# Context values of a cross-attention block: one VectorE subtraction for three GpSimd ones

## The reference

```python
x = x + attention(layernorm(x), ctx, ctx)      # ctx: (8, 375, 512)
x = x + experts(layernorm(x))

def attention(x, k_cache, v_cache):
    q, k_new, v_new = x @ wq.T, x @ wk.T, x @ wv.T
    k = concat([k_cache, k_new]); v = concat([v_cache, v_new])
    attn = softmax(q @ k.T * 512**-0.5)
    return (attn @ v) @ wo.T

def experts(x):                                 # gate: softmax, top 2 of 8, renormalised
    for gu, dp, w in (gate_up_proj, down_proj, combine_w):
        gate, up = split(x @ gu.T, 2)
        acc += w * ((silu(gate) * up) @ dp.T)
```

## Time and profile before

| | us |
|---|---|
| median of 3 runs | 463.65 |
| lowest and highest run | 462.8, 464.78 |
| the profiled execution's own time | 463.22 |
| its span, from the first to the last instruction | 461.4 |

### The profile page before, as it was taken

How to read it: one execution, slowest core, us unless ns; L and a number is a source line. 1 busy time by engine, 2 the same in 40 slices (tenths; PEclk the granted TensorE clock), 3 DMA queues, 4 the chain that set the end, 5 groups by cost and what they waited for, 6 DMA issues and landing times.

```text
span 461.4 us, 7183 instructions
## 1 busy us (share of the span) xinstructions
PE 443.8 (96%) x2549; PEld 376.0 (82%) x2549; DVE 346.2 (75%) x653; ACT 251.7 (55%) x409; POOL 95.8 (21%) x122
## 2 busy tenths in 40 slices
PE   8899999999999899999999999999999999999991
PEld 6878888888888578888888888888888888888870
DVE  5856646556644577998888888888888888888850
ACT  3648434524533536656656656656656656656621
POOL 4005071552425424003003003003003003003002
PEclk9999999999999999999999999999999999999996
DMA  8975994505544464955956946856856946856203
GB/s 237 396 229 150 290 238 138 167 23 145 195 137 189 123 224 115 344 199 200 268 172 194 277 167 200 270 166 202 269 168 200 276 161 220 264 160 201 40 1 51
DMA packets 26912, 88.40 MB, mean 192 GB/s; under 512 B 2560, under 2 KB 8704, under 8 KB 26880
## 3 DMA queue, kind: packets, MB, share of 16 engines
q1 hardware_dynamic: 23296, 80.13, 53.1%
q0 software_dynamic: 3584, 7.88, 8.3%
HBM read 73.55 MB, written 14.45 MB: 191 GB/s over the span
## 4 chain that ended last, share of the span: by engine, by line
PE 89%; DVE 4%; ACT 2%; POOL 1%; DMA 1%; issue 0%; POOLq 0%; SPq 0%; DVEq 0%; ACTq 0%
PE PJ L340 13%; PE T L340 13%; PE PJ L341 7%; PE T L341 7%; PE SC L228 4%; PE SC L230 4%; PE SC L229 4%; PE SC L413 3%; PE SC L412 3%; PE SC L411 3%; PE PJ L228 3%; PE PJ L230 3%; PE PJ L229 3%; PE T L236 3%; PE R L411 2%; PE R L412 2%
## 5 line engine op out<-in xcount | busy, mean ns | idle before, releaser
L750 DVE TENSOR_TENSOR ul<-ng,uh 128x1536 fp32r<-128x1536 f32 x64 | 112.5, 1758 | 3.1 <-ACT uh L536 2.1
L536 ACT ACTIVATE uh<-ng 128x1536 fp32r<-128x1536 f32 x64 | 94.6, 1480 | 0.0
L340 PE MATMUL PJ<-eb,uh 128*128 128x512 f32 x256 | 91.5, 397 | 0.1
L340 PE MATMUL T<-eb,uh 128*128 128x512 f32 x256 | 91.5, 397 | 0.0
L341 PE MATMUL PJ<-eb,ul 128*128 128x256 f32 x256 | 72.0, 281 | 0.0
L341 PE MATMUL T<-eb,ul 128*128 128x256 f32 x256 | 71.9, 281 | 0.0
L1170 POOL DMA_INDIRECT out<-ys,yidx x16 | 27.8, 1740 | 196.7 <-ACT ys L689 194.3
L340 PEld LDWEIGHTS PJ<-eb,uh 128*128 128x128 f32 x256 | 48.1, 188 | 11.7 <-issue 0.3
L340 PEld LDWEIGHTS T<-eb,uh 128*128 128x128 f32 x256 | 48.1, 188 | 11.5
L341 PEld LDWEIGHTS T<-eb,ul 128*128 128x128 f32 x256 | 48.3, 189 | 1.3
L341 PEld LDWEIGHTS PJ<-eb,ul 128*128 128x128 f32 x256 | 48.3, 189 | 1.3
(11 more groups left out here) (206 smaller groups left out, 924.6 us busy)
## 6 DMA issues: line engine op xcount, KB each, us to landing
ng<-in_units SPq DMA_DIRECT2D x64, 768.0 KB, 4.3
vs<-in_ctxn SPq DMA_DIRECT2D x8, 768.0 KB, 4.9
kTs<-in_ctxT SPq DMA_DIRECT2D x8, 750.0 KB, 4.9
slots<-zero SPq DMA_DIRECT2D x8, 514.0 KB, 11.6
xe<-slots SPq DMA_DIRECT2D x8, 514.0 KB, 4.3
wTs<-in_weights SPq DMA_DIRECT2D x8, 512.0 KB, 9.4
out<-x_all SPq DMA_DIRECT2D x8, 224.0 KB, 3.7
x_all<-in_x SPq DMA_DIRECT2D x1, 896.0 KB, 18.0
```

The costliest lines, as they stand in the source:

```text
L340: nc.tensor.matmul(o[:, :].rearrange("p (h s) -> p h s", h=2), wh, both[:, k, :, :], start=k == 0, stop=False)
L536: nc.scalar.activation(o, i, ACT.Copy).then_inc(s, 1)
L750: v.tensor_tensor(o, whole, hi.bitcast(F32), ALU.subtract).then_inc(s, 1)
```

## The change

The rest of the context's values is made by VectorE. One instruction takes the three blocks of a batch at once, 128 rows by 1536 numbers, instead of three of 512 on GpSimd; the last block's nine rows of padding are now computed too. `lo_v` of batch A stands between `norm_x` (in bodies 0 and 3, `lo_a` of batch A) and `do_max` of batch B, and `lo_v` of batch B ahead of `inv` and `lo_a` of batch B. Both are done in the body that uses them, and no longer in the one before. `v_lo` is raised once for a batch, and the attention product waits once, ahead of its first block. The amount of work on TensorE, ScalarE and SyncE, and its order, are the same. The expert part is not touched.

```diff
@@ pe_attn
+            pe.wait_ge(v_lo, g + 1)
             for j, n in enumerate(CROWS):
-                pe.wait_ge(v_lo, 3 * g + j + 1)
                 nc.tensor.matmul(o, aTh[a][0:n, j + 1, :], vh[a][0:n, j, :], start=False, stop=False)
@@ vector
+            def lo_v(g, a):
+                dve.wait_ge(v_hi, g + 1)
+                lo(vl[a][:, :, :], vs[a][:, :, :], vh[a][:, :, :], v_lo)
@@ vector, body
                 lo_a(A, 0, T[0])
                 if p and more:
                     norm_x(p + 1)
+                lo_v(A, 0)
                 do_max(B, 1)
...
                 if p and more:
                     topk(p - 1)
+                lo_v(B, 1)
                 inv(B, 1)
                 lo_a(B, 1, T[0])
@@ gpsimd
-            def lo_v(g, a):
-                pool.wait_ge(v_hi, g + 1)
-                for j, n in enumerate(CROWS):
-                    g_.tensor_tensor(vl[a][0:n, j, :], vs[a][0:n, j, :], vh[a][0:n, j, :].bitcast(F32),
-                                     ALU.subtract).then_inc(v_lo, 1)
@@ gpsimd, body
-                if p == 0:
-                    lo_v(0, 0)
-                    lo_v(1, 1)
-                else:
+                if p:
                     weights(p - 1)
...
                 rstd_x2(A, 0)
                 rstd_x2(B, 1)
-                if more:
-                    pool.wait_ge(x2_norm, B + 1)
-                    lo_v(A + 2, 0)
-                    lo_v(A + 3, 1)
```

## The result

| | before | after |
|---|---|---|
| median of the runs compared, us | 464.21 (4 runs) | 470.89 (4 runs) |
| lowest and highest | 462.8, 465.06 | 470.0, 471.86 |
| the profiled execution's own time | 463.22 | 471.73 |
| its span | 461.4 | 470.0 |

The ratio is 1.0145, with a 95% interval of 1.0111 to 1.0178. The change is slower, as forecast, but 470.89 lies above the stated range (466.2 to 470.5). The page of the changed kernel shows the work moved: VectorE's busy time rose from 346.2 us to 357.8, somewhat less than by eight times 1.67 (the `kTl` of 2.29 us in the earlier trace rows is back at 1.72, for one), and GpSimd's fell from 95.8.

A forecast was written before the change was run, and what follows sets the result against it. The prediction took TensorE's own work to bound bodies 1 and 2, so every wait adds to the end. Terms 0.34 + 2 x (1.93 + 0.1) + 0.45 + 0.25 = 5.1 us on 463.22 gave 468.3, taken as 468.5; range 466.2 to 470.5.

The forecast's parts named there:

- One instruction, 1.75 us long and 1.67 to the next: Each new VectorE subtraction takes 1.75 us, next instruction 1.67 after its start; eight add 13.4 us of VectorE work.
- Bodies 1 and 2, 1.93 each, 0.66 of it at projection 0: TensorE waits 0.66 us for `xTl` at projection 0; lateness at B's attention product totals 1.93 us per body.
- Body 0, 0.34: Body 0: 0.66 us won from GpSimd waits is lost to the later row maximum; B's `aTl` leaves +0.34 us.
- Body 3, 0.45, and 0.25 for contention: Body 3: B's late `aTl` costs 0.45 us; GpSimd's power instruction overlapping `lo_v` of A costs 0.25 more.
- the 0.1 each: Bodies 1 and 2: contention of GpSimd's power instruction with `lo_v` of B, ends 0 and 0.73, taken as 0.1 us.
- `early`, ends 0 and 0.5, I took 0: After body 3: later GpSimd scatters delay the load of `early`; TensorE's wait for it 0 to 0.5 us, taken as 0.
- the bodies' sum, 5.1 forecast: All four bodies: 0.34 + 2 x (1.93 + 0.1) + 0.45 + 0.25 = 5.1 us lost.
- The transport to the time: Whole kernel: 5.1 us added to one execution's 463.22 gives 468.3, taken as 468.5; no new waits elsewhere.
- only one of the two places costs: Rival for bodies 1 and 2: first delay of 1.03 us absorbed, 0.9 lost per body, 466.4 us; chance 0.14.
- the subtractions fit into idle time: Rival for the bodies: VectorE's idle time takes the work and GpSimd waits go, not slower, 462.6 or 463.5 us; chance 0.08.
- Contention decides: Rival: GpSimd's small instructions beat `lo_v` of B each time and `early` is 0.5 us late, 470.3 us; chance 0.14.

The follow-up runs named there:

- best: Changed kernel with bodies 1 to 3's subtractions moved to VectorE idle time, and body 0's too, after an earlier ScalarE copy: 463.22 us beside 463.94, ratio 0.9993.
- the repeat: The changed kernel measured once more, no edit, against the kernel before: 468.92 us beside 463.94, ratio 1.0106.
- late_filled: Kernel before plus 1.45 us of extra VectorE work in the start and 14 idle products on TensorE between projections 1 and 2: 464.67 us, ratio 1.0018.
- gaps: Changed kernel with the subtractions of bodies 1 to 3 moved into VectorE idle time at the end of the body before: 464.56 us, ratio 0.9998.
- late: Kernel before plus 1.45 us of extra VectorE work in the start, no idle products: 467.10 us beside 464.09, ratio 1.008.

## Why the prediction was wrong

- *One instruction, 1.75 us long and 1.67 to the next*: right, eight times.
- *Bodies 1 and 2, 1.93 each, 0.66 of it at projection 0*: right to 0.01 in both profiles of the changed kernel and in its parts.
- *Body 0, 0.34*: 0.33 and 0.35. The 0.66 that was won from GpSimd and lost at once to the later maximum is shown by best, which keeps it.
- *Body 3, 0.45, and 0.25 for contention*: 0.51 up to L274; `vl` wasn't stretched. In bodies 1 and 2 the 0.1 each weren't there either.
- *`early`, ends 0 and 0.5, I took 0*: 0.35 in the first profile, and in the second TensorE waits 0.34 for it. This term was under-sized: the scatters were later by more than TensorE was. It makes up for the contention, so that the bodies' sum, 5.1 forecast, was 5.03 and 5.16: in part luck.
- *The transport to the time*: this is the step that failed. I wrote "No transfer, nor the expert part, has a new wait: 0" and added the sum to 463.22, one execution whose start was good, with a range made of the change's own unknowns. In the first measurement's profile the start added 3.17 us: 1.55 for a late transfer, 1.62 for the lower clock behind TensorE's wait. A term for the start was missing. Such runs aren't rare: in 18 of 113 runs of kernels without idle products and without the work added by hand the mean clock is 0.991 or less, and in before such runs lie 1.8 to 3.6 us above the median of the others.

That the late start doesn't belong to the change rests on three things: the repeat, whose difference is 4.98 us and whose profiled start lost 0.52; late_filled, which is made from the kernel before and whose profile has the same late transfer and the same fall of the clock; and the kernel before itself, which has slow runs with a low mean clock in 9 of 59, though where their clock fell wasn't seen. That clock and start explain the first set isn't shown in full: two of its four runs, 471.73 and 471.86, have the clock of 0.989, and the other two, at 470.0 and 470.05 with 0.995 and 0.993, are 1.1 us above the median of the repeat's five runs at such a clock (468.9) and 0.2 above the highest of them (469.76). No profile of them exists; that 1 us stays open. A late first transfer could give it without any fall of the clock: in gaps's profile the first `wTh` started at 8.15 us instead of 6.63, and the start took 33.14 us instead of 31.64. That start of before, on whose execution the forecast was laid, is the shortest of all twelve profiles.

Of the rivals, "only one of the two places costs" and "the subtractions fit into idle time" are refuted for the change as written, though the second holds for other places in the same bodies (gaps, best). "Contention decides" is refuted by the changed kernel's own profile, in which each `vl` took 1.75 or 1.76 us; of its 0.5 for `early` 0.35 came.

The Trainium skill ("SBUF — State Buffer", section on the two separate sides) says that a VectorE operation with two SBUF inputs and a GpSimd one that reads SBUF exclude each other, whichever starts first winning. In body 1 after the change it agrees from the other side: `vl` started at 81.87 and GpSimd's power instruction at 82.07, and the latter took 2.14 us instead of 0.73:

```profile
82.07 2.14 POOL L1128 TENSOR_TENSOR xr<-el,minus 112x2 f32<-112x2 f32 x1
```

In body 3 the order was turned round, GpSimd first by 0.34 us, and VectorE still wasn't held up; the instruction behind on GpSimd was, 1.34 us for 0.20. There the measurement decides: a GpSimd instruction on 112x2 that had already begun cost VectorE nothing that the profile shows.

## What to carry to other kernels

When one engine is the bound without a gap, price work added elsewhere by its place: the slack between each result and the bound engine's need of it, read from two start times, minus what the new instruction uses up; costs of two places don't add up where they share a slack. Moving the same work into idle time ahead of instructions that wait anyway made 5.2 us of loss into none. And before a forecast is laid on one execution's time, look at how its start compares with other runs: a range made only of the change's own unknowns leaves out what the unchanged part does from run to run.

## What the hardware showed that I had not expected

- TensorE waited 2.40 us in one run and then had a clock of 0.53 and 0.62 in the two stretches behind it; it waited 2.55 us at the same place in another (late) and kept 1.00, and 2.39 us in a third (late_filled) with 0.50 behind it. What decides isn't shown.
- Eight idle products in a wait of 1 us cost nothing that can be measured, and in 16 runs with them no mean clock of 0.991 or less occurred. At the rate of 18 in 113 that would happen by chance in about 6 of 100 cases (an estimate), so that they help isn't shown. Fourteen of them didn't prevent the fall when the wait lasted 2.39 us beyond them.
